# A layer's first group gathers 18 rows on TensorE in three rounds, and 46 on GpSimd

## The reference

```
alpha = leaky_relu(a_src[src] + a_dst[dst])        # layer 2: times edge_weight first
amax  = segment_max(alpha, dst);  alpha = exp(alpha - amax[dst])
denom = segment_sum(alpha, dst)
out   = segment_sum(xh[src] * (alpha / denom[dst]), dst)
```

## Time and profile before

| | |
|---|---|
| median of the runs | 4196.76 us |
| the profiled execution | 4206.04 us, its span 4204.3 us |
| TensorE matmul busy | 2835.5 us, 67% |
| VectorE busy | 3093.4 us, 74% |
| ACT busy | 2404.4 us, 57% |
| GpSimd busy | 2674.2 us, 64% |
| granted TensorE clock | 0.843 of full speed |
| attention layers in the span | first turn (L1530) at 1083, 2152 and 3226 us, last one at 1937, 3021 and 4079 us |

### The profile page before, as it was taken

How to read it: one execution, slowest core, us unless ns; L and a number is a source line. 1 busy time by engine, 2 the same in 40 slices (tenths; PEclk the granted TensorE clock), 3 DMA queues, 4 the chain that set the end, 5 groups by cost and what they waited for, 6 DMA issues and landing times. The chain is left out here.

```text
span 4204.3 us, 58554 instructions
## 1 busy us (share of the span) xinstructions
PE 2835.5 (67%) x16208; PEld 1804.7 (43%) x16208; DVE 3093.4 (74%) x9684; ACT 2404.4 (57%) x5241; POOL 2674.2 (64%) x2801
## 2 busy tenths in 40 slices
PE   1899998985476676765456766757625667676773
PEld 1344445543354453544333544535423445354543
DVE  6999994564577676778656777867864767676787
ACT  1888882005466665663555666656545666566654
POOL 5766660305777777774477777777437777777753
PEclk7999999996788888887578888888857889888887
DMA  3111112542232222221123223322103222222221
GB/s 104 56 83 83 56 83 83 223 152 57 64 68 69 68 64 69 69 69 35 46 65 70 70 70 70 70 64 71 41 22 73 69 69 65 68 68 69 68 45 31
DMA packets 127620, 298.57 MB, mean 71 GB/s; under 512 B 45412, under 2 KB 74972, under 8 KB 123712
## 3 DMA queue, kind: packets, MB, share of 16 engines
q0 software_dynamic: 74976, 155.58, 16.3%
q1 hardware_dynamic: 52320, 139.24, 9.8%
HBM read 241.28 MB, written 53.38 MB: 70 GB/s over the span
## 5 line engine op out<-in xcount | busy, mean ns | idle before, releaser
L1416 POOL DMA_INDIRECT work<-table,lane_src x2184 | 2101.3, 962 | 665.9 <-issue 648.3
L1513 PE MATMUL psum<-work 128*128 128x396 bf16 (+1 forms) x5850 | 1162.0, 354 | 66.3 <-ACT work L1458 31.1
L1455 ACT ACTIVATE work<-work,middle_node_number 128x384 f16<-128x384 f16 x1587 | 954.4, 601 | 221.6 <-PE psum L1513 201.0
L1458 ACT ACTIVATE work<-work 128x384 bf16<-128x384 f16 x1587 | 829.8, 523 | 50.5
L1570 PE MATMUL psum<-work 128*128 128x136 f32 x4836 | 702.2, 303 | 186.5 <-DVE work L1701 95.6
L1513 PEld LDWEIGHTS psum<-work 128*128 128x128 bf16 x5850 | 597.1, 104 | 510.5 <-issue 120.6
L1570 PEld LDWEIGHTS psum<-work 128*128 128x128 f32 x4836 | 654.2, 208 | 272.5 <-issue 159.2
L1738 DVE TENSOR_TENSOR node_sums<-node_sums,psum 128x136 f32 x2418 | 558.8, 293 | 102.3 <-PE psum L1570 95.2
L793 POOL TENSOR_SCALAR work<-work 128x128 f16<-128x128 f16 x392 | 333.8, 852 | 221.8 <-PE psum L808 194.5
L771 DVE TENSOR_SCALAR work<-work 128x400 f16<-128x400 f16 x1568 | 463.6, 318 | 0.7 <-PEq L667 0.6
L741 PE MATMUL psum<-work 128*128 128x448 f16 x2100 | 454.3, 354 | 3.2 <-PEq L1166 2.5
(11 more groups left out here) (374 smaller groups left out, 2930.1 us busy)
## 6 DMA issues: line engine op xcount, KB each, us to landing
counts<-work SPq DMA_DIRECT2D x14, 2800.0 KB, 8.6
work<-counts SPq DMA_DIRECT2D x14, 2800.0 KB, 10.0
work<-table,lane_src POOLq DMA_INDIRECT x2184, 2.5
work<-spread SPq DMA_DIRECT2D x78, 256.0 KB, 4.1
work<-masks SPq DMA_DIRECT2D x78, 128.0 KB, 3.0
work<-source_rows SPq DMA_DIRECT2D x39, 192.0 KB, 3.8
spread<-node_sums SPq DMA_DIRECT2D x4, 896.0 KB, 9.2
table<-work SPq DMA_DIRECT2D x10, 330.0 KB, 2.9
```

Source lines behind the costliest of these rows:

```text
L1416: pool.indirect_dma_start(m.ring[:, s % SLOTS, 0:F + H], None, m.d_table[H], bass.IndirectOffsetOnAxis(ap=m.src[:, s:s + 1], axis=0)).then ...
L1455: act.activation(away, rows_of(g, u), ACT.Abs, bias=m.low_tile[:, hi:hi + 1]).then_inc(far_known, 1)
L1458: act.activation(hot_of(g, u), away, ACT.Relu, bias=1.0, scale=-1.0).then_inc(hot_act, 1)
L1513: mm = pe.matmul(aid_banks[:, k, 0:3 * (F + H)], hot_of(g, u)[:, k * P:(k + 1) * P], m.all_thirds[:, :, hi, 0:F + H], start=(hi == 0), sto ...
```

## The change

In the first group of a layer TensorE does three rounds of six steps. The other groups are as before. Rounds are now counted by themselves: rounds 0 to 2 belong to group 0, and round g + 2 to a later group g. GpSimd leaves out the first 18 steps of the layer in place of six, so it gathers 716 steps in a layer and not 728. ACT makes the even hots of all three rounds before it starts on the six of group 1, VectorE the odd ones. The spread of group 0 moves from behind the round into the third one: VectorE does it in front of unit 20 and TensorE turns it behind its unit 11. SP issues the source numbers of the first two rounds before the wait for the spread values, and those of the third behind them.

```diff
+SPREAD_FROM = 12
+FIRST_ROUNDS = 3
...
     def gathered(b):
-        return [s for s in steps_of(b) if place(s) >= AIDED]
+        return [s for s in steps_of(b) if place(s) >= AIDED * (FIRST_ROUNDS if s < lo_of(1) else 1)]
...
+    def round_of(g):
+        return FIRST_ROUNDS - 1 + g
+
+    def round_lo(r):
+        return r * AIDED if r < FIRST_ROUNDS else lo_of(r - FIRST_ROUNDS + 1)
...
         @block.sync
+            def aid_rows(r):
+                if r >= 2:
+                    sp.wait_ge(hot_used, (r - 1) * UNITS)
+                lo = round_lo(r)
+                sp.dma_start(m.aid_rows[r % 2], m.d_src_rows[lo:lo + AIDED, :].rearrange("(a s) e -> a (s e)", a=1)
+                             .to_broadcast([P, AIDED * P])).then_inc(aid_rows_in[r % 2], 16)
...
-                if g >= 2:
-                    sp.wait_ge(hot_used, (g - 1) * UNITS)
-                sp.dma_start(m.aid_rows[g % 2], m.d_src_rows[own.start:own.start + AIDED, :].rearrange("(a s) e -> a (s e)", a=1)
-                             .to_broadcast([P, AIDED * P])).then_inc(aid_rows_in[g % 2], 16)
+                if g == 0:
+                    for r in range(min(2, FIRST_ROUNDS)):
+                        aid_rows(r)
+                else:
+                    aid_rows(round_of(g))
...
+                if g == 0:
+                    for r in range(2, FIRST_ROUNDS):
+                        aid_rows(r)
...
         @block.scalar
-            for u in range(0, UNITS, 2):
-                hot_on_act(0, u)
+            for r in range(FIRST_ROUNDS):
+                for u in range(0, UNITS, 2):
+                    hot_on_act(r, u)
             for u in range(CHAIN_HOTS[0]):
-                hot_on_act(1, u)
+                hot_on_act(round_of(1), u)
...
-                        act.wait_ge(aid_taken, (g + 1) * PASSES)
+                        act.wait_ge(aid_taken, (round_of(g) + 1) * PASSES)
...
         @block.tensor
-            aid(0, range(UNITS))
+            for r in range(FIRST_ROUNDS - 1):
+                aid_round(r, range(UNITS))
+            aid(0, range(SPREAD_FROM))
             turn_spread(0)
+            aid(0, range(SPREAD_FROM, UNITS))
...
         @block.vector
-            for u in range(UNITS):
-                if u % 2:
-                    hot_on_dve(dve, 0, u)
-                if u % NODE_TILES == NODE_TILES - 1:
-                    take_aided(0, u // NODE_TILES)
-            spread(0)
+            for r in range(FIRST_ROUNDS):
+                for u in range(UNITS):
+                    if u % 2:
+                        hot_on_dve(dve, r, u)
+                    if r == FIRST_ROUNDS - 1 and u == SPREAD_FROM + 7:
+                        spread(0)
+                    if u % NODE_TILES == NODE_TILES - 1:
+                        take_aided(r, u // NODE_TILES)
             onehot(0)
             onehot(1)
```

More of the change, by code:

```diff
@@ L1375, in parts_of, with made_by_dve, made, hot_of @@
         return range(b - blocks[0], len(part_of) if b == blocks[-1] else b - blocks[0] + 1)
[L1377 to L1381, removed]
+    def round_of(g):
+        return FIRST_ROUNDS - 1 + g
+    def round_lo(r):
+        return r * AIDED if r < FIRST_ROUNDS else lo_of(r - FIRST_ROUNDS + 1)
+    def made_by_dve(r, u):
+        return u % 2 == 1 if r < FIRST_ROUNDS else u in by_dve
+    def made(r, u):
+        return sum(made_by_dve(k, v) == made_by_dve(r, u) for k in range(r + 1) for v in range(UNITS if k < r else u + 1))
     def tails_of(g):
         return sum(1 + (lo_of(k) % SLOTS + size_of(k) > SLOTS) for k in range(g + 1))
[L1386 to L1393, removed]
+    def hot_of(r, u):
+        return m.aid_hot[(r * UNITS + u) % HOTS]
+    def rows_of(r, u):
+        return m.aid_rows[r % 2][:, u // NODE_TILES * WIDE_HOT:(u // NODE_TILES + 1) * WIDE_HOT]
+    def wait_for_hot(eng, r, u):
+        n = r * UNITS + u
         if n >= HOTS:
             eng.wait_ge(hot_used, n - HOTS + 1)
[L1396 to L1400, removed]
+        if u == 0 or r < FIRST_ROUNDS or u in by_dve:
+            eng.wait_ge(aid_rows_in[r % 2], 16 * (r // 2 + 1))
+    def hot_on_dve(dve, r, u):
+        wait_for_hot(dve, r, u)
         hi = u % NODE_TILES
         odd = lambda view: view.rearrange("p (a e) -> p a e", a=3)
-        dve.tensor_scalar(odd(hot_of(g, u)), odd(rows_of(g, u)), m.tile_low[:, hi:hi + 1], None, ALU.is_equal).then_inc(hot_dve, 1)
+        dve.tensor_scalar(odd(hot_of(r, u)), odd(rows_of(r, u)), m.tile_low[:, hi:hi + 1], None, ALU.is_equal).then_inc(hot_dve, 1)
     def halves(view):
@@ L1449, in _, with hot_on_act @@
             far = [0]
-            def hot_on_act(g, u):
-                wait_for_hot(act, g, u)
+            def hot_on_act(r, u):
+                wait_for_hot(act, r, u)
                 hi = u % NODE_TILES
                 away = m.aid_far[far[0] % 2]
-                act.activation(away, rows_of(g, u), ACT.Abs, bias=m.low_tile[:, hi:hi + 1]).then_inc(far_known, 1)
+                act.activation(away, rows_of(r, u), ACT.Abs, bias=m.low_tile[:, hi:hi + 1]).then_inc(far_known, 1)
                 far[0] += 1
                 act.wait_ge(far_known, far[0])
-                act.activation(hot_of(g, u), away, ACT.Relu, bias=1.0, scale=-1.0).then_inc(hot_act, 1)
-            for u in range(0, UNITS, 2):
-                hot_on_act(0, u)
+                act.activation(hot_of(r, u), away, ACT.Relu, bias=1.0, scale=-1.0).then_inc(hot_act, 1)
+            for r in range(FIRST_ROUNDS):
+                for u in range(0, UNITS, 2):
+                    hot_on_act(r, u)
             for u in range(CHAIN_HOTS[0]):
-                hot_on_act(1, u)
+                hot_on_act(round_of(1), u)
             for g in range(GROUPS):
@@ L1477, in _ @@
                     for u in range(CHAIN_HOTS[0], AHEAD_HOTS):
-                        hot_on_act(g + 1, u)
+                        hot_on_act(round_of(g + 1), u)
                 act.wait_ge(exponents, g + 1)
@@ L1496, in _ @@
                         if u not in by_dve:
-                            hot_on_act(g + 1, u)
+                            hot_on_act(round_of(g + 1), u)
                 if g + 2 < GROUPS:
                     for u in range(CHAIN_HOTS[0]):
-                        hot_on_act(g + 2, u)
+                        hot_on_act(round_of(g + 2), u)
         @block.tensor
@@ L1504, in aid, with aid_round @@
             def aid(g, units):
-                if g >= GROUPS:
-                    return
+                if g < GROUPS:
+                    aid_round(round_of(g), units)
+            def aid_round(r, units):
                 for u in units:
                     n, hi = divmod(u, NODE_TILES)
-                    pe.wait_ge(hot_dve if made_by_dve(g, u) else hot_act, made(g, u))
-                    if hi == 0 and g * PASSES + n:
-                        pe.wait_ge(aid_taken, g * PASSES + n)
+                    pe.wait_ge(hot_dve if made_by_dve(r, u) else hot_act, made(r, u))
+                    if hi == 0 and r * PASSES + n:
+                        pe.wait_ge(aid_taken, r * PASSES + n)
                     for k in range(PER_BANK):
-                        mm = pe.matmul(aid_banks[:, k, 0:3 * (F + H)], hot_of(g, u)[:, k * P:(k + 1) * P], m.all_thirds[:, :, hi, 0:F + H],
+                        mm = pe.matmul(aid_banks[:, k, 0:3 * (F + H)], hot_of(r, u)[:, k * P:(k + 1) * P], m.all_thirds[:, :, hi, 0:F + H],
                                        start=(hi == 0), stop=(hi == NODE_TILES - 1))
@@ L1708, in onehot, with take_aided @@
                                   over(m.drel[:, b * U:b * U + n].unsqueeze(2), [P, n, P]), ALU.is_equal).then_inc(hot, 1)
-            def take_aided(g, n):
+            def take_aided(r, n):
                 third = [aid_banks[:, :, i * (F + H):(i + 1) * (F + H)] for i in range(3)]
-                lo = lo_of(g) + n * PER_BANK
+                lo = round_lo(r) + n * PER_BANK
                 rows = slots(lo, PER_BANK)[:, :, 0:F + H]
-                dve.wait_ge(hot_used, g * UNITS + (n + 1) * NODE_TILES)
+                dve.wait_ge(hot_used, r * UNITS + (n + 1) * NODE_TILES)
                 if lo >= SLOTS:
@@ L1719, in take_aided @@
                 dve.tensor_tensor(rows, rows, third[0], ALU.add).then_inc(aid_taken, 1)
-                dve.wait_ge(aid_taken, g * PASSES + n + 1)
+                dve.wait_ge(aid_taken, r * PASSES + n + 1)
             def places_of(lo, n):
@@ L1761, in _ @@
                             if u in by_dve:
-                                hot_on_dve(dve, g + 1, u)
+                                hot_on_dve(dve, round_of(g + 1), u)
                     if n:
@@ L1765, in _ @@
                     if g + 1 < GROUPS and n in TAKEN_IN:
-                        take_aided(g + 1, TAKEN_IN.index(n))
+                        take_aided(round_of(g + 1), TAKEN_IN.index(n))
                 add_up(blocks[-1], False)
@@ L1770, in _ @@
                     spread(g + 1)
-                    take_aided(g + 1, PASSES - 1)
```

(1 more changed line is left out.)

## The result

The changed kernel takes 4153.38 us (median of five runs, 4151.87 to 4156.54) against 4196.76; the ratio is 0.9899, its interval 0.9887 to 0.9910. The forecast was 4154. The profiled execution took 4152.9 us, its span 4151.1.

What follows compares the result with a forecast made beforehand. The prediction took GpSimd's gathers to bound each layer: 45.4 us saved by removed gathers, less a 2.3 us slot wait, gave -43.1 us, so 4196.8 becomes 4154; range 4149 to 4169.

Steps and rivals of the forecast that it cites:

- Gathers bound a layer: GpSimd's 728 gathers set a layer's length; removing twelve a layer saves 15.1 us each, 45.4 us over three layers.
- Turn 0 later: TensorE's turn of group 0's score columns comes 31.9, 36.9 and 32.6 us later in layers 1, 2 and 3.
- Given back: Later groups need about 61 us without gather waits, not 73, so the late start is recovered well before group 10.
- Slot wait in layer 2 alone: Group 2's gathers reuse group 0's ring slots; GpSimd waits 2.3 us in layer 2, none in layers 1 and 3.
- Product 16: Second sixteen of L1570 in group 0, whose slot the 107th gather needs; ends 22.9, 25.5 and 21.6 us behind turn 0.
- Free edits: SP's reordered source-row loads and shifted counters cost nothing; if the cover failed, turn 0 moves up to 4 us.
- rival B: VectorE's 50 more hots a layer hold GpSimd, costing 15.2 us a layer, whole gain lost: about 4197; chance 0.03.
- Sum: Whole program: -45.4 + 2.3 = -43.1 us; profiled execution 4206.0 to 4162.9, median of the runs 4154.

Runs made afterwards that it cites:

- the gathers kept: Three rounds as in the changed kernel, but GpSimd also gathers the 12 rows into slots overwritten later: 4195.08 us against 4194.19 before, ratio 1.0002.
- the table: Gathers removed x 1.255 us, less slot waits, against measured gain over before, for eight kernels; the sum is within 3 us in every row.
- second profile of before: The kernel before, unchanged, profiled once more: 4195.06 us, median gather 944 ns against 947 in the first profile.
- other two measurements: The changed kernel run again beside other kernels: 4149.68 us (ratio 0.9890) and 4153.50 us (0.9897) against before.
- four rounds: Four rounds in group 0 instead of the change's three, 40 gathers there: 4233.31 us, ratio 1.0097 against before.
- two sets of banks: The changed kernel with TensorE's passes alternating between two sets of PSUM banks, VectorE taking one while the next runs: 4150.18 us, ratio 0.9891 against before.

## Why the prediction was right, point by point

- **Gathers bound a layer**: shown. With the gathers kept nothing changed; in the other kernels of the table the gain followed their number, less the slot waits.
- **Turn 0 later**: right, with a size off. I had 106.6, 111.6 and 107.3 us behind the first gather and it was 102.1, 112.8 and 103.6. The term is the period of a pass. I took 16.64 for all four (17.05 in layer 2). In layer 1 they went 14.68, 16.64, 17.29 (with the spread's stop in it) and 16.64: a pass that TensorE ran at full clock throughout has 12.72 us of matmuls, not 14.42. The 16.64 was one sample: in the second profile of before the same period was 15.02. The stop cost 2.6 against my 3.0 in layer 1, and 4.3 in layer 2.
- **Given back**: right. 59 to 61 us a group (61 said), 62.6 to 65.4 in layer 2 (64.5 said); done by turn 4, and by turn 5 in layer 2.
- **Slot wait in layer 2 alone**: right in place, 4.7 us where I had 2.3. Two terms were off. Product 16 ended 138.2 us behind the first gather, where I had 137.1, since turn 0 came 1.2 later:

```profile
2191.77 2.02 PE L1595 MATMUL psum<-work 128*128 128x136 f32 x16
```

  And the 107th gather did not keep its time: it was due at 133.8 us and not at 134.8, since the 106 gathers before it took 0.9 us less in sum than in before. The 105th gather's wait adds nothing of its own; without it the 107th would have waited the whole 4.7. In another execution of the same kernel it was 1.5. The margin of layers 1 and 3 was wider than I had it.
- **Free edits**: nothing that the runs with the gathers kept can tell.
- **VectorE holds GpSimd** (rival B): not so. In the first 100 us of layers 1 and 2 the windows of L1424, and then of L1411, are

```profile
1003.89:1104.26 100.37, 76.22 (x80) 0.92 0.31 73
2055.58:2166.62 111.04, 84.22 (x89) 0.87 0.33 77
...
1003.89:1104.26 100.37, 22.79 (x75) 0.92 0.31 73
2055.58:2166.62 111.04, 22.61 (x75) 0.87 0.33 77
```

  80 gathers in 100.4 us beside 75 hots, 1.255 each. In the whole trace 410 gathers ran while VectorE was making a hot (L1411), and none of them took over 1.05 us. By the rule of the Trainium skill (SBUF — State Buffer, "Who interferes with whom"), if the hots run in a two-port mode, which the trace doesn't tell, they could have held the gathers of layer 1's window for up to 22.8 us (an estimate: the time of its hots); this trace does not show it.
- **Sum**: 43.1 predicted, 43.4 measured. That they are so close is luck: with its own slot wait of 4.7 the sum is 40.5, and the same kernel gained 46.4 and 42.9 in its other two measurements. What I said of the profiled execution was wrong: it went from 4206.0 to 4152.9, not to 4162.9. The first profile of before lay 9 us over its median, and I carried that over to the changed kernel, though it belonged to one execution. The forecast of the median doesn't hang on it.
- **Open**: between two profiles with the same median gather (0.944 us) the change won 41.3 us in the layers with a sum of 40.5, but layers 1 and 3 won 1 us less than twelve gathers, layer 2 with its waits 3 more. Lengthened gathers account for most of it. What they took over 0.944 us each adds up to 5.4, 20.8 and 5.5 us in the layers of before (second profile) and to 6.5, 18.6 and 7.0 in the change: 1 to 1.5 us more in layers 1 and 3, 2 less in layer 2. They lie beside some operations of VectorE: in the change 53 of the 106 gathers beside the spread's scans (L1622) took over 1.05 us, and 4 of the 473 beside `message` (L1726). That is where they lie, not a cause; no run took one of these operations away.

## What to carry to other kernels

When one queue sets the length of a stage, work taken off it counts in full, even at the price of a start that is 30 us later, as long as the rest of the stage is faster per step than the queue; read that slack from the trace (from one step's start to the point where only the queue's result is missing) and not from busy shares. Then look for what the queue needs back from the late part: here a ring slot. Below that point a late start costs nothing that these runs can tell (15 us earlier gained nothing), above it one for one (four rounds lost), and that point, not the gathers saved, says how much can be moved.

## What the runs showed of the hardware

TensorE's clock fell behind some gaps and not behind others of nearly the same length: behind 2.22 us it fell and behind 1.95 it did not, but in another profile of the changed kernel (the one beside two sets of banks) it fell behind 1.96 (a pass of 14.40 us), and in the second profile of before it did not behind 2.28 (12.74 us). Two passes of layer 1 of the changed kernel, the stretches behind these gaps, with the granted clock behind the count of matmuls:

```profile
1040.00:1043.00 3.00, 3.00 (x20) 1.00 0.63 171
...
1055.00:1058.00 3.00, 3.00 (x11) 0.50 0.19 45
```

At 1.00 (2.4 GHz) a pass took 12.72 us, with some 3.4 us at 0.50 (1.2 GHz) 14.42; in layer 1 of this profile they alternated, in the one beside two sets they did not (12.74, 14.40, 14.42), and in layer 2 those without the stop were all of the slower kind, 14.8 us. With two sets of banks and no gap, 333 matmuls ran in 58.38 us, 175 ns each; a pass with the fall has 192, one at 1.00 throughout 170. A period measured once, as I did, can be the better or the worse kind.
